# Opening of a convolution tower: order of constants, loads and stores of round 0, and its first pairs

## The reference

```
CONVS = [(128, 10, 5)] + [(128, 3, 2)] * 4 + [(128, 2, 2)] * 2      # channels, taps, stride
h = x[:, None, :]
for w, g, b, s in zip(conv_ws, ln_gs, ln_bs, strides):
    h = conv1d(h, w, s); h = gelu(layernorm over channels(h) * g + b)
h = h + attention(layernorm(h));  h = h + experts(layernorm(h))
```

## Time and profile before

| | us |
|---|---|
| median of 3 runs | 904.41 |
| lowest, highest | 904.39, 908.73 |
| the profiled execution | 903.9 |
| its span, first to last instruction | 901.8 |
| TensorE busy in the span | 752.5 (83%) |
| VectorE busy | 640.3 (71%) |
| ScalarE busy | 331.3 (37%) |
| GpSimd busy | 313.0 (35%) |
| mean granted TensorE clock | 0.923 |

### The profile page before, as it was taken

How to read it: one execution, slowest core, us unless ns; L and a number is a source line. 1 busy time by engine, 2 the same in 40 slices (tenths; PEclk the granted TensorE clock), 3 DMA queues, 4 the chain that set the end, 5 groups by cost and what they waited for, 6 DMA issues and landing times. The chain is left out here.

```text
span 901.8 us, 11857 instructions
## 1 busy us (share of the span) xinstructions
PE 752.5 (83%) x4259; PEld 574.4 (64%) x4259; DVE 640.3 (71%) x1447; ACT 331.3 (37%) x562; POOL 313.0 (35%) x365
## 2 busy tenths in 40 slices
PE   0039999999999999999787578788888888899987
PEld 0016565565655665665554477768788887899977
DVE  3946867887788966546646566998888888553387
ACT  0034456354544564454313215113333231346333
POOL 3003320412231312222100006475788787238301
PEclk9999978999799988998989589989999999989999
DMA  1360150006100330000000070000000000200000
GB/s 60 45 133 1 35 115 1 1 1 124 26 1 1 62 76 0 1 1 1 1 0 1 1 323 2 1 1 1 1 1 1 2 1 1 80 1 1 1 1 26
DMA packets 22564, 25.48 MB, mean 28 GB/s; under 512 B 17052, under 2 KB 21212, under 8 KB 21404
## 3 DMA queue, kind: packets, MB, share of 16 engines
q1 hardware_dynamic: 22508, 24.74, 11.2%
HBM read 21.05 MB, written 3.66 MB: 27 GB/s over the span
## 5 line engine op out<-in xcount | busy, mean ns | idle before, releaser
L457 POOL TENSOR_TENSOR diff<-h 128x400 f32<-128x400 f32 x112 | 97.6, 895 | 300.0 <-ACT h L562 135.1
L536 PEld LDWEIGHTS ps<-averager,sq 128*100 128x100 f32 (+2 forms) x1024 | 103.2, 176 | 16.7 <-ACT sq L579 8.1
L499 PE MATMUL ps<-h,w 128*128 128x400 f32 x224 | 109.9, 620 | 1.3 <-ACT h L584 0.5
L536 PE MATMUL ps<-averager,sq 128*100 128x1 f32 (+2 forms) x1024 | 101.1, 229 | 4.0 <-ACT sq L579 3.9
L682 DVE TENSOR_TENSOR h<-ps,shared 128x800 f32<-128x800 f32 x56 | 55.4, 989 | 57.2 <-PE ps L508 53.8
L579 ACT ACTIVATE sq<-h 128x800 f32<-128x800 f32 (+1 forms) x58 | 50.1, 864 | 118.7 <-DVE h L682 112.6
L508 PE MATMUL ps<-diff,w 128*128 128x400 f32 x224 | 91.1, 528 | 0.0
L1023 PE MATMUL pt<-for_pe,ident 128*128 128x156 f32 (+2 forms) x420 | 67.0, 318 | 23.4 <-DVE for_pe L1222 23.4
L562 ACT ACTIVATE h<-ps,lnp 128x800 f32<-128x800 f32 x64 | 63.5, 1014 | 47.5 <-PE ps L476 47.1
L1023 PEld LDWEIGHTS pt<-for_pe,ident 128*128 128x128 f32 x420 | 60.7, 196 | 28.5 <-DVE for_pe L1222 26.1
L476 PE MATMUL ps<-late,w_stack 90*128 90x400 bf16 x128 | 35.9, 383 | 49.1 <-DMA late<-windows_dram 45.0
(11 more groups left out here) (283 smaller groups left out, 1369.4 us busy)
## 6 DMA issues: line engine op xcount, KB each, us to landing
late<-windows_dram SPq DMA_DIRECT2D x24, 375.0 KB, 7.6
gate_w<-in_gate_w SPq DMA_DIRECT2D x1, 3456.0 KB, 14.0
up_w<-in_up_w SPq DMA_DIRECT2D x1, 3456.0 KB, 19.3
windows_dram<-parts SPq DMA_DIRECT2D x12, 250.0 KB, 5.4
acts<-in_down_w SPq DMA_DIRECT2D x1, 1728.0 KB, 8.1
w<-in_w SPq DMA_DIRECT2D x1, 1024.0 KB, 5.3
xs<-in_x SPq DMA_DIRECT2D x4, 252.5 KB, 4.7
out_tokens<-hidden SPq DMA_DIRECT2D x6, 96.0 KB, 1.6
```

The lines of the kernel that those rows point to most:

```text
L457: pool.tensor_tensor(to[:, rows, :], here[:, rows, :], behind[:, rows, :], ALU.subtract).then_inc(diff_ready, 1)
L499: pe.matmul(out[:, c, :, :], w[:, L.first_tap + 1, :], plane(l, s, p, 1, slice(c, L.pos, 2)), start=True, stop=False)
L536: mm = pe.matmul(var_ps[0:L.w, at:at + 1], sq[:, square_of[r, l, s, p] % 2, c, q * L.w:(q + 1) * L.w], averager[:, 0:1], start=True, stop= ...
```

## The change

- TensorE no longer waits for all constants and weights before its products of the taps, but for the averager and `w0` alone, and for the first identity matrix before its transposition. `w0` is loaded ahead of the samples, with a semaphore of its own. GpSimd makes the identity matrix ahead of spreading the phases, its other constants behind. The wait for all 14 constants stands behind the tap products.
- The samples of round 1 are loaded ahead of round 0's stores.
- Round 0's stores are cut in two: lanes 0 to 63 and 64 to 127 of each part (six DMAs). When the three first halves have landed, four pieces are read back, then the other half's. A piece is two clips, all 90 rows in one DMA of 3200 bytes a row, whose source names the 30 stored rows three times by a leading dimension of 3 with step 0. `first` in round 0 waits for its own piece.
- A new list `FIRST_ORDER` stands ahead, behind the spreading of round 1's phases and its prep 0 to 3. The steps in it are taken out of their old places.

```diff
--- before.py
+++ after.py
...
     +prep.0.0.2 var.3.0.0 +first.0.0.2 half.3.1.0 norm.3.0.0 conv.3.1.0 +half.1.0.0 +prep.0.0.3 rows.3.0.0
 """
 
+FIRST_ORDER = """
+    first.0.0.0 first.0.0.1 half.1.0.0 first.0.0.2 first.0.0.3 conv.1.0.0 prep.0.0.4 half.1.0.1 first.0.0.4 first.0.0.5 conv.1.0.1
+    var.1.0.0 prep.0.0.5 half.1.0.2 first.0.0.6 first.0.0.7 conv.1.0.2 var.1.0.1 prep.0.0.6 half.1.0.3 first.0.1.0 conv.1.0.3
+    var.1.0.2 prep.0.0.7 prep.0.0.8 first.0.1.1 prep.0.0.9 var.1.0.3
+"""
+
 LAST_ORDER = """
     half.4.0.0 conv.4.0.0 half.4.0.1 var.4.0.0 conv.4.0.1 half.4.1.0 var.4.0.1 norm.4.0.0 conv.4.1.0 half.4.1.1 rows.4.0.0
     scale.4.0.0 scale.4.0.1 gelu.4.0.0 var.4.1.0 conv.4.1.1 scale.4.0.2 scale.4.0.3 gelu.4.0.1 half.5.0.0 var.4.1.1 norm.4.1.0
...
 
 def tower_plan():
 
-    order = []
+    order, started = [], []
+    for what, _, l, s, p in steps_of(FIRST_ORDER):
+        started.append((what, int(what == "prep"), l, s, p))
     for turn in range(-1, ROUNDS + 1):
         for what, later, l, s, p in steps_of(ROUND_ORDER):
             r = turn + later
...
                 order.append((what, r, l, s, p))
     for what, _, l, s, p in steps_of(LAST_ORDER):
         order.append((what, ROUNDS - 1, l, s, p))
+    opening = [x for x in order if x[0] in ("prep", "phases") and x[1] == 1 and (x[0] == "phases" or x[4] < 4)]
+    assert len(opening) == 5 and set(started) <= set(order)
+    order = opening + started + [x for x in order if x not in opening + started]
     return counted(order)
 
 
...
+        MEAN, IDENT, CONSTS = 1, 3, 14
+
...
                     sp.wait_ge(parts_out, 16 * PARTS * (r + 1))
                     return scratch
 
+                def first_windows():
+
+                    scratch = windows_dram[0, :, :]
+                    half = P // 2
+                    for a in range(PARTS):
+                        sp.wait_ge(parts_ready, a + 1)
+                        for slot, done in enumerate((first_out, parts_out)):
+                            to = scratch[a * K0:(a + 1) * K0, slot * half * SL:(slot + 1) * half * SL]
+                            sp.dma_start(to.rearrange("k (l t) -> l k t", t=SL),
+                                         parts[slot * half:(slot + 1) * half, a, :, :]).then_inc(done, 16)
+                    for slot, done in enumerate((first_out, parts_out)):
+                        sp.wait_ge(done, 16 * PARTS)
+                        for i in range(GROUP // 2):
+                            piece = slot * GROUP // 2 + i
+                            cut = slice(2 * piece * POS0, 2 * (piece + 1) * POS0)
+                            rows = scratch[:, cut]
+                            thrice = bass.AP(rows.tensor, rows.offset, [[0, PARTS], [ROUND * POS0, PARTS * K0], [1, 2 * POS0]])
+                            sp.dma_start(win[:, cut], thrice).then_inc(win_piece[piece], 16)
+
                 def back(scratch, slot):
                     cut = slice(slot * GROUP * POS0, (slot + 1) * GROUP * POS0)
                     for a in range(PARTS):
                         sp.dma_start(win[a * PARTS * K0:(a + 1) * PARTS * K0, cut], scratch[:, cut]).then_inc(win_in[slot], 16)
 
+                sp.dma_start(w0[:, :], io["w0"]).then_inc(w0_here, 16)
                 samples(0)
-                sp.dma_start(w0[:, :], io["w0"]).then_inc(w_in, 16)
                 sp.dma_start(lnp[:, :], io["lnp"]).then_inc(w_in, 16)
                 sp.dma_start(w[:, :, :], io["w"]).then_inc(w_in, 16)
 
...
                     for b in range(PARTS):
                         row = (a * PARTS + b) * K0
                         sp.dma_start(w0_stack[row:row + K0, :], w0_parts[:, a, :]).then_inc(w0_in, 16)
-                scratch = windows(0, True)
-                back(scratch, 0)
-                back(scratch, 1)
+                sp.wait_ge(phases_ready, 1)
+                samples(1)
+                first_windows()
                 attention_weights(sp, io, res)
 
                 for r in range(1, ROUNDS):
...
                     pool.tensor_copy(phases[:, :, :], xs[:, :].rearrange("p (t k) -> p k t", k=STRIDE0)).then_inc(phases_ready, 1)
 
                 pool.memset(averager[:, :], 1.0 / CH).then_inc(s_const, 1)
+                pool.memset(ident[:, :], 0.0).then_inc(s_const, 1)
+                pool.wait_ge(s_const, IDENT - 1)
+                pool.affine_select(out=ident[:, :], in_=ident[:, :], compare_op=ALU.not_equal, fill=1.0, base=0,
+                                   pattern=[[-1, P]], channel_multiplier=1).then_inc(s_const, 1)
                 spread_phases(0)
-                pool.memset(ident[:, :], 0.0).then_inc(s_const, 1)
                 pool.memset(ident16[:, :], 0.0).then_inc(s_const, 1)
                 pool.memset(pick[:, :, :], 0.0).then_inc(s_const, 1)
                 pool.memset(rparts[:, :, :, :], 0.0).then_inc(s_const, 1)
...
                 pool.memset(h1[:, :, :, :, L1.pos // 2:L1.row // 2], 0.0).then_inc(s_const, 1)
                 pool.memset(h2[:, :, :, :, L2.pos // 2:L2.row // 2], 0.0).then_inc(s_const, 1)
                 pool.memset(h3[:, :, :, :, :, L3.pos // 2:L3.row // 2], 0.0).then_inc(s_const, 1)
-                pool.wait_ge(s_const, 4)
-                for m in (ident, ident16):
-                    pool.affine_select(out=m[:, :], in_=m[:, :], compare_op=ALU.not_equal, fill=1.0, base=0,
-                                       pattern=[[-1, P]], channel_multiplier=1).then_inc(s_const, 1)
+                pool.wait_ge(s_const, 6)
+                pool.affine_select(out=ident16[:, :], in_=ident16[:, :], compare_op=ALU.not_equal, fill=1.0, base=0,
+                                   pattern=[[-1, P]], channel_multiplier=1).then_inc(s_const, 1)
 
                 for a in range(PARTS):
                     if a:
...
                             rows = slice(half * n, half * n + n)
                             pool.tensor_tensor(to[:, rows, :], here[:, rows, :], behind[:, rows, :], ALU.subtract).then_inc(diff_ready, 1)
 
-            CONSTS = 14
             SLOT_IN = 16 * PARTS
 
             @block.tensor
             def _(pe):
 
 
-                pe.wait_ge(s_const, CONSTS)
-                pe.wait_ge(w_in, 48)
+                pe.wait_ge(s_const, MEAN)
+                pe.wait_ge(w0_here, 16)
                 pe.matmul(spread[0][:, 0:K0], averager[:, :], w0[:, :], start=True, stop=True).then_inc(s_w0, 1)
                 pe.wait_ge(s_w0, 3)
                 pe.matmul(spread[1][:, 0:K0 * K0], averager[:, :], w0_pairs[:, :, :], start=True, stop=True).then_inc(s_w0, 1)
+                pe.wait_ge(s_const, IDENT)
                 pe.transpose(ps[0:K0, 6, 0:CH], w0[:, :], ident[:, :]).then_inc(weights_ready, 1)
 
                 def first(b, bank):
...
                                        win[:, b * POS0 + h:(b + 1) * POS0:2], start=True, stop=True)
                     mm.then_inc(y_ready, 1)
 
+                pe.wait_ge(s_const, CONSTS)
                 pe.wait_ge(w0_in, 16 * PARTS * PARTS)
 
                 for what, r, l, s, p, n in plan:
...
                         else:
                             pe.wait_ge(y_copied, number + 1)
                     if what == "first":
-                        pe.wait_ge(win_in[s], SLOT_IN * (r + 1))
+                        if r == 0:
+                            pe.wait_ge(win_piece[(s * GROUP + p) // 2], 16)
+                        else:
+                            pe.wait_ge(win_in[s], SLOT_IN * r)
                         first(s * GROUP + p, n["bank"])
                     elif what == "half" and l in PAIRED:
                         if n["conv"] == 0:
...
 
             @block.scalar
             def _(act):
-                act.wait_ge(w_in, 48)
+                act.wait_ge(w_in, 32)
 
                 def first(s, p, b, pair):
                     act.wait_ge(y_ready, pair + 1)
                     act.activation(h0[:, s, p, :, 0:POS0 // 2], ypair[b][:, :, 0:400],
                                    ACT.Gelu, scale=lnp[:, 0:1], bias=lnp[:, 1:2]).then_inc(y_taken, 1)
 
-                act.wait_ge(s_const, CONSTS)
+                act.wait_ge(s_const, IDENT)
 
                 act.activation(warm[:, :], ident[:, 0:1], ACT.Gelu)
                 for what, r, l, s, p, n in plan:
...
                         steps.settle()
                         if r > 0:
                             dve.wait_ge(parts_out, 16 * PARTS * r)
+                        if r == 1:
+                            dve.wait_ge(first_out, 16 * PARTS)
                         nc.vector.tensor_copy(parts[:, 0, :, :], scaled_win[:, :, :]).then_inc(parts_ready, 1)
                         dve.wait_ge(parts_ready, PARTS * r + 1)
                     else:
...
                 for part in range(PREP):
                     prepare(0, part)
 
-                dve.wait_ge(w_in, 48)
+                dve.wait_ge(w_in, 32)
                 steps.done(nc.vector.tensor_reduce(wmean[:, :], w[:, :, :], AX.X, ALU.add))
```

(3 more changed lines are left out.)

## The result

The changed kernel took 901.27 us (median of 20 runs, 897.37 to 904.66) against 905.71 (20 runs) before: ratio 0.9948, 95% interval 0.9932 to 0.9964, so by the ratio 4.7 us faster, where 8.2 were forecast. The profiled execution's span fell from 901.8 to 897.4 us.

What follows compares the result with a forecast made beforehand. The prediction held TensorE busy after an opening that nothing hides; an earlier start and reading back, less GpSimd's disturbance and the new order's cost, put half.1.1.0 8.2 us earlier: 904.4 - 8.2 = 896.2, rounded to 896, range 889 to 904.

Steps and rivals of the forecast that it cites:

- start: Opening up to the preparation: TensorE's first product at 3.5 instead of 12.31, everything up to the preparation 8.8 us earlier.
- GpSimd beside VectorE: Sample preparation on VectorE: GpSimd's constants now run beside it and cost 3.5 us, bounds 0 to 5.75.
- round 1's phases: Last four preparation steps: GpSimd's spreading of round 1's phases now falls there and adds 1.0 us, bounds 0 to 1.1.
- stores: From the last part to reading back: 4.9 us instead of 7.1, reading back at 41.25, bounds 3.9 to 7.1.
- first piece: Reading back: 2.0 fixed plus 3.75 us on three engines, first piece landed at 47.0.
- the new order: From half.1.0.0 to half.1.1.0: more convolutions 0 and waits for GELUs add 7.9 us to 23.2, bounds 5 to 11.
- The row of one for one: Profile row behind the GpSimd term: three 128x100 VectorE steps came through beside three GpSimd differences in 2.26 us.
- theory 1: Stores, forecast for whole_stores: bound by their 3840 runs of 200 bytes; reading back at 43.4 to 43.9, ratio 0.995.
- the bound, 11: Upper bound of the new order's 7.9 us: TensorE runs part of the stretch as slowly as the first half.
- B: Rival on pieces and preparation: pieces on many engines, or less GpSimd disturbance; 893 us, both together 890; chance 0.22.
- C: Rival on pieces: three engines at 13.6 GB/s, 7.1 us a piece, half.1.1.0 at 101.6, whole 917 us; chance 0.13.
- D: Rival behind the opening: gain lost as TensorE waits for round 1's windows; 901 to 904.5 us; chance 0.20.

Runs made afterwards that it cites:

- quiet: Changed kernel with GpSimd's other constants and the spreading of round 1's phases moved behind the last preparation step; ratio to the kernel before 0.9888.
- whole_stores: Changed kernel with each part stored by one DMA of 128 lanes instead of two of 64; ratio to the kernel before 0.9974.
- rows_outermost: Changed kernel with the 30 stored rows outermost and the step of 0 behind, later rounds read back by one such DMA per slot; ratio to before 0.9940.
- combined: Changed kernel with quiet, rows_outermost and the previous pair's var between a pair's two convolutions 0; 891.12 us, ratio to before 0.9846.
- old_order_slots: Changed kernel, but read back by slots with three DMAs of 30 rows each and the old order of steps; ratio to the kernel before 0.9954.
- late_start: Changed kernel, but TensorE waits for all constants, identity matrix made behind the phases, taps loaded behind the samples; ratio to the kernel before 1.0019.
- combined_loud: combined with whole stores, but with GpSimd's constants beside the preparation as in the changed kernel; 896.21 us, ratio to the kernel before 0.9905.

## Why the prediction was wrong

The direction held and the mechanisms were there, but the gain was little more than half of the forecast: four of its six terms were mis-sized to the same side. At half.1.1.0, forecast 8.25 earlier, measured 3.7:

| step | forecast | measured | loss |
|---|---|---|---|
| start: first product earlier by | 8.8 | 9.7 | -0.9 |
| GpSimd beside VectorE | 3.5 | 5.85 | 2.35 |
| round 1's phases | 1.0 | 0.8 | -0.2 |
| stores, from the last part to reading back | 4.9 | 5.8 | 0.9 |
| first piece, to the first convolution 0 | 5.75 | 6.76 | 1.0 |
| the new order, added to 23.2 | 7.9 | 9.3 | 1.4 |

The 5.85 is the first product's 9.70 less the 3.85 by which the two-input steps began earlier (17.46 to 13.61; 17.46 is the end of the earlier trace rows's 15.54 + 1.88 with its handover). 4.0 of it fell ahead of the preparation, 1.8 in its first ten steps. The start gained because `w0` had landed 1.8 us after its issue (0.81 to 2.61), where I took 2.7.

- **GpSimd beside VectorE** is the step that failed most. I put the first disturbed instruction at 6.75, at the preparation, and overlooked the taps' own casts at 5.4, which stand beside the memsets: one took 3.47 and the step behind it 1.08. The row of one for one was of two-input steps beside differences that read; beside constants VectorE got nothing through for 3 us. By the Trainium skill (SBUF — State Buffer, section Who interferes with whom) casts and single-input steps may take both port pairs of VectorE, one of them shared with GpSimd, and then a GpSimd instruction that came first holds them up, a plain write too. The cast of 3.47 beside memsets agrees; the prediction had applied this to the ten single-input steps and not to the cast. quiet shows the whole of it: 6.3 us with the phases.
- **Stores.** I took the least landing time for granted because the queue would be short. The stores took about the same time whatever came: reading back began 9.7, 9.9 and 10.8 us after the first store was issued, in the changed kernel, whole_stores and quiet, 10.3 before, and 9.3 to 10.8 over all the runs, however the parts came and whether they were halved. Whether their 3840 runs of 200 bytes bind them, as my theory 1 has it, or their 768 KB, no run separates.
- **Pieces.** Three engines, as I took it, and about 3.75 a piece: 96 KB x 3 in that time is 77 GB/s, and the stretch from 53 to 61 shows 77, 25.7 an engine. The Trainium skill's rule (DMA: Bandwidth & Descriptors, section Rules for kernel authors) of at most c engines for a leading broadcast of c copies was right, and rows_outermost, where the broadcast is not leading, confirms it. What I missed is the fixed part, by difference 3.0 (6.76 less 3.75) instead of 2.0: the rows had it for a DMA of 30 rows issued in 0.4, this one takes 0.7 to issue. The other 0.7 is not explained.
- **Order.** Pairs 1 and 2 came out as forecast: 6.95 and 7.00 us, 1.7 more than before, for one more convolution 0 and the wait for a GELU (the idle times are 1.11 to 1.15). The miss is in pair 0 and in the last stretch, 0.7 us each, and it is TensorE's pace. Pair 0 needed 7.89 us (53.04 to 60.93), with matmuls at half pace (3.00 for four, 1.53 for the next two) though the granted clock reads 1.00. Ahead of half.1.1.0 four matmuls of convolution 0 took 1.49 where others take 0.87, and there the granted clock itself had fallen, to the lower of its two levels, 0.50, from 83 on. TensorE had been busy without a gap from 75 to 80, at 1.00 (columns as in the earlier trace rows):

```profile
75.00:80.00 5.00, 5.00 (x27) 3.15 (x27) 1.84 (x6) 2.04 (x3) 0.07 (x1) 1.00 0.15 56
80.00:83.00 3.00, 2.72 (x23) 2.15 (x23) 2.90 (x9) 1.78 (x2) 1.07 (x1) 0.85 0.00 0
83.00:86.00 3.00, 2.50 (x7) 0.83 (x6) 2.90 (x4) 2.35 (x3) 1.35 (x2) 0.50 0.00 0
```

In whole_stores, with the same list and 0.99 granted, the order cost 7.85 (31.08 less 23.23), the forecast's 7.9. I had the bound, 11, and didn't take it seriously.
- **Rivals.** B's many engines (0.18 of them busy) and C's slow ones (25.7 GB/s each) are out. D, a gain lost behind the opening, isn't seen in the change's pair of traces (811.8 against 812.5), but in part in combined. It isn't excluded as a small term: the kernels with the new list had a mean granted clock of 0.914 to 0.919, before beside them 0.920 to 0.923 and old_order_slots 0.921, and time goes with it (before took 901.1 us in an execution at 0.928, 911.0 in one at 0.915).

The forecast credited pieces and order together with 1.7 us (8.25 less the 6.5 by which reading back was to start earlier). The runs show no sign of it, though the ratios could not tell 1.7 us from nothing: old_order_slots has the same ratio without them, and late_start, which has them without the early start, is not faster than before. What a first pair 9 us sooner brings, the waits for GELUs and six more convolutions 0 take back: these used to run ahead of the dense stretch, beside 2.8 us in which TensorE waited for the second slot's windows anyway, and now stand inside it. From the trace of before:

```profile
61.16 1.49 PE L476 MATMUL ps<-late,w_stack 90*128 90x400 bf16 x4 [2.80 <-DMA late<-windows_dram]
```

## What to carry to other kernels

Starting the first dense step sooner is worth only what isn't paid back in the dense stretch: compare the start of the last step that the new order touches, not of the first. A constant or copy on GpSimd that is moved out of an idle time of VectorE must be charged for everything that VectorE runs beside it, from the first instruction on; put it behind the critical part instead. When two short steps share a buffer, put an independent one between them in the order of every engine that follows the same list.

## What the runs showed of the hardware that I had not expected

SyncE was held while its DMAs on three engines ran. The line of the pieces (issue lengths in ns, of eight):

```profile
L420 SPq DMA_DIRECT2D late<-windows_dram x8: 677/745/6086, 43.3 to 56.9; - x8
```

One issue lasted 6.1 us where the median is 0.75, and SyncE was bound until 60.7; on 15 engines all eight were issued in 6.9, none over 0.88. That a long issue waits for room behind the earlier pieces is my reading, which no run tests. The attention's weights, next on SyncE, were issued at 60.8 instead of 50.4; the first matmul that uses one of them starts at 526.6. Issue itself depends on the shape: 0.4 us for a store of 128 lanes (before and whole_stores), 0.65 for one of 64 lanes.

Whole executions of one kernel lie up to 11 us apart (901.5 to 912.5 in 24 of before). From half.1.1.0 to the end, where TensorE's order is the same in all, the traces need 809.4 us (old_order_slots) to 819.0 (combined_loud), so a trace's own end says less than its opening.
